# Two shared blocks' gate products moved into the units of the last sequence, and the gather indices computed first

## The reference, cut to what matters

```python
x = x + xattn(layernorm(x), ctx)          # 16 sequences of 128 channels x 512
# xattn: 8 heads of 16, keys within 64 places of the query, softmax, out projection, relu,
#        times ctx, mixing of the channels
xt = layernorm(x)                         # 2048 tokens (rows) of 512
top2 of softmax(xt @ Wr.T + bias)         # 16 experts, weights normalised
routed = sum over the two experts e of w * (silu(xt @ Wg[e]) * (xt @ Wu[e])) @ Wd[e]
shared = silu(xt @ sWg) * (xt @ sWu) @ sWd
out = x + routed + shared
```

## Time and profile before

| what | value |
|---|---|
| median of 3 runs | 713.51 us (709.81 to 713.77) |
| the profiled execution's own time | 713.82 us |
| its span, first to last instruction | 712.1 us |
| TensorE busy | 656.3 us, 92% of the span |
| GpSimd, VectorE, ScalarE busy | 432.8, 390.1, 358.8 us |
| TensorE's mean granted clock | 0.976 of full speed |

### The profile page before, as it was taken

The page is one execution under the profiler, slowest core; times in us unless marked ns, Lnnn a source line. Parts: engine busy times, 40 slices in busy tenths (PEclk is TensorE's granted clock), DMA queues, the critical chain, the costliest instruction groups (busy, mean ns, idle before and its releaser), DMA issues. The chain is left out here.

```text
span 712.1 us, 13863 instructions
## 1 busy us (share of the span) xinstructions
PE 656.3 (92%) x4070; PEld 318.3 (45%) x4070; DVE 390.1 (55%) x1424; ACT 358.8 (50%) x673; POOL 432.8 (61%) x653
## 2 busy tenths in 40 slices
PE   3679999999999999998899999899999999999992
PEld 1345545555555555554444444333333333333330
DVE  3778888888888888861224786322222222222220
ACT  4237777777777777665323101344444344444441
POOL 5238788888888887777310001257867677767663
PEclk9968999999999999998999999999999999999997
DMA  6533545655444444311498944435555566544430
GB/s 204 161 105 91 143 123 164 167 161 151 129 133 139 135 137 137 103 49 50 127 401 342 418 161 149 133 78 108 118 132 107 147 121 128 119 96 88 80 50 0
DMA packets 67579, 99.45 MB, mean 140 GB/s; under 512 B 18601, under 2 KB 43305, under 8 KB 65449
## 3 DMA queue, kind: packets, MB, share of 16 engines
q1 hardware_dynamic: 52848, 70.68, 32.0%
q0 software_dynamic: 9600, 18.89, 14.4%
q10 hardware_dynamic: 5058, 8.99, 3.7%
HBM read 50.99 MB, written 23.33 MB: 104 GB/s over the span
## 5 line engine op out<-in xcount | busy, mean ns | idle before, releaser
L1175 DVE CUSTOM_DVE_ANT_0 bank<-bank,cb 128x192 f32<-128x192 f32 (+1 forms) x512 | 185.8, 415 | 35.5 <-PE bank L580 35.1
L954 ACT ACTIVATE wgu<-bank 128x384 f32<-128x384 f32 (+1 forms) x256 | 125.7, 548 | 45.8 <-PE bank L598 45.2
L785 PE MATMUL bank<-wgu,rowsT 128*64 x320 | 145.9, 599 | 0.0
L787 PE MATMUL bank<-X,rowsT 128*64 128x512 f32 x320 | 145.9, 598 | 0.0
L1408 DVE TENSOR_TENSOR act_in<-act_in,bank 128x256 f32<-128x256 f32 x56 | 23.5, 420 | 194.9 <-ACT act_in L1070 173.5
L580 PE MATMUL bank<-wgu 96*128 96x192 bf16 (+1 forms) x512 | 96.3, 274 | 19.1 <-DVE wgu L1175 14.4
L466 POOL TENSOR_SCALAR_AFFINE_SELECT wgu<-wgu 128x512 f32<-128x512 f32 (+1 forms) x128 | 74.9, 585 | 49.0 <-ACT wgu L954 49.0
L512 POOL DMA_INDIRECT rows<-xn_rows,gather_i x40 | 44.2, 1106 | 84.5 <-DVE gate_of L1403 58.5
L530 POOL DMA_INDIRECT out<-y_out,scatter x40 | 64.2, 1605 | 37.7 <-DMA out<-y_out,scatter_i 23.1
L530 POOL DMA_INDIRECT out<-y_out,scatter_i x40 | 64.3, 1606 | 30.8 <-issue 22.1
L580 PEld LDWEIGHTS bank<-wgu 96*128 96x128 bf16 x512 | 45.8, 102 | 80.4 <-issue 38.6
(11 more groups left out here) (174 smaller groups left out, 1088.8 us busy)
## 6 DMA issues: line engine op xcount, KB each, us to landing
wgu<-wgu SPq DMA_DIRECT2D x190, 128.0 KB, 2.7
wgu<-w_gu SPq DMA_DIRECT2D x16, 1024.0 KB, 14.1
X<-w_d SPq DMA_DIRECT2D x16, 512.0 KB
out<-y_out ACTq DMA_DIRECT2D x17, 256.0 KB, 4.1
X<-x SPq DMA_DIRECT2D x16, 256.0 KB, 3.3
wgu<-ctx SPq DMA_DIRECT2D x16, 256.0 KB, 3.3
xn_rows<-xn SPq DMA_DIRECT2D x16, 256.0 KB, 2.4
xn_turned<-xn2T SPq DMA_DIRECT2D x16, 256.0 KB, 3.4
```

The lines of the kernel that those rows point to most:

```text
L785: mm(gb[k.buf][0:GROUP, :], rowsT[:, k.buf, c, 0:GROUP], wgu[:, bass.ds(e * 2048 + 512 * c, 512)], start=(c == 0), stop=(c == 3))
L787: last = mm(gb[k.buf][GROUP:P, :], rowsT[:, k.buf, c, GROUP:P], gu_half[:, k.buf, 512 * c:512 * c + 512], start=(c == 0), stop=(c == 3))
L954: nc.scalar.activation(probs[j % 4][:, 2 * half:2 * half + 2, 0:w], s2[half][:].rearrange("p (j c) -> p j c", j=2)[:, :, 0:w], ACT.Exp, sc ...
L1175: last = v.tensor_tensor_reduce(o, o, cb[:, B_MASK + off:B_MASK + off + w], 1.0, MASKED * 2.0, ALU.add, ALU.max, rowmaxes[n % 2][:, h + i, ...
```

## The change

Four gate and up products for each of blocks 0 and 1 go into the units U = 129 to 136, one product behind each unit's own work (`soon_gate_up`), into the two banks `s1`, which the score products have left by then. Their SiLU stands at U = 139 and 140, and their `activate` at U = 140 on VectorE. Units 141 to 158 then drain blocks 2 to 7 as they drained blocks 0 to 5, and take the transposes and the down products of blocks 0 and 1 as well. Behind the units eight shared blocks are left where there were ten. The loads of rows start five units before U = 129. The stores of blocks 0 and 1 are issued at i = 4 and 5 behind DRAIN where block 0's was at 7. The gather indices are computed ahead of `places_and_orders` and have a semaphore of their own, `gather_ready`. The first `turn_rows` of the routed blocks, which stood inside the last `pe_step`, stands behind the last `turn_act`, and the second stands behind the last `down`.

The diff, cut to its core:

```diff
-DRAIN, DRAINED = UNITS * (SEQS - 1) + 20, 6
+DRAIN, DRAINED, SOON = UNITS * (SEQS - 1) + 20, 8, 2
+FIRST_SOON = DRAIN - 11
...
-            pool.wait_ge(tables_ready, 1)
+            pool.wait_ge(gather_ready, 1)
...
             for j in range(AHEAD):
                 gather(j)
+            pool.wait_ge(tables_ready, 1)
             pool.wait_ge(spare_stored, 16)
...
+                if 0 <= U - FIRST_SOON < 4 * SOON:
+                    soon_gate_up(*divmod(U - FIRST_SOON, 4))
+                if DRAIN < U <= DRAIN + 3 * (DRAINED - SOON):
+                    third = (U - DRAIN - 1) % 3
+                    drain_shared((U - DRAIN - 1) // 3 + SOON, third)
+
+            def soon_gate_up(b, c):
+
+                k = Turn(b, 0, 2)
+                if b == 0 and c == 0:
                     pe.wait_ge(rowmax, 2 * UNITS * SEQS)
                     pe.wait_ge(shared_in, 96)
...
+                if c == 0:
+                    pe.wait_ge(rows_in[k.n % 3], 16 * (k.n // 3 + 1))
+                last = mm(s1[b][:], rows[:, k.n % 3, P * c:P * c + P], swgu[:, c, :], start=(c == 0), stop=(c == 3))
...
             def drain_shared(b, third):
 
                 k = Turn(b, 0, 2)
                 if third == 0:
-                    if b == 0:
+                    if b == SOON:
                         pe.wait_ge(exp_ready, 2 * UNITS * SEQS)
+                    if b == SOON + 1:
+                        down(Turn(1, 0, 2), s1[1])
                     half_gate_up(k, 0)
                 elif third == 1:
-                    if b == 1:
+                    if b == SOON:
                         pe.wait_ge(o_copied[0], SEQS)
                         pe.wait_ge(o_copied[1], SEQS)
-                    if b > 0:
+                        turn_act(Turn(0, 0, 2))
+                        turn_act(Turn(1, 0, 2))
+                    else:
                         turn_act(k.plus(-1))
                     half_gate_up(k, 1)
-                elif b > 0:
+                elif b == SOON:
+                    down(Turn(0, 0, 2), s1[0])
+                else:
...
-                if U == DRAIN - 4:
+                if U == FIRST_SOON - 5:
                     act.wait_ge(turned_stored, 48)
                     for k in range(3):
                         load_rows(Turn(k, 0, 2))
...
+            def rows_to_gather():
 
                 dve.wait_ge(table_mm, 4)
                 link(v.tensor_copy(table, rb[:, AT_TABLE:AT_TABLE + TABLE]))
-                part = lambda g: table[:, g * BLOCKS:(g + 1) * BLOCKS]
                 link(v.scalar_tensor_tensor(slot[:, 0, :], part(0), float(P), part(1), ALU.mult, ALU.add))
+                v.tensor_scalar(gather_i[:], slot[:, 0, :], -1.0, 0.0, ALU.add, ALU.max).then_inc(gather_ready, 1)
...
             result(Turn(DRAINED + 5, 0, 2))
+            rows_to_gather()
             places_and_orders()
             routing_tables()
             activate(Turn(DRAINED + 7, 0, 2))
             result(Turn(DRAINED + 6, 0, 2))
-            for k in range(DRAINED + 8, SEQS):
-                activate(Turn(k, 0, 2))
-                result(Turn(k - 1, 0, 2))
-                if k == SEQS - 2:
-                    dve.wait_ge(y_ready, SEQS - 4)
-                    copy_half(Turn(SEQS, 0, 2))
+            dve.wait_ge(y_ready, SEQS - 4)
+            copy_half(Turn(SEQS, 0, 2))
             result(Turn(SEQS - 1, 0, 2))
```

More of the change, by code:

```diff
@@ L879, in _ @@
             turn_act(Turn(SEQS - 1, 0, 2))
+            turn_rows(Turn(SEQS, 0, 2))
+            down(Turn(SEQS - 1, 0, 2))
             turn_rows(Turn(SEQS + 1, 0, 2))
-            down(Turn(SEQS - 1, 0, 2))
             pe.wait_ge(experts_in, 16 * EXPERTS)
@@ L1021, in drain_shared @@
             def drain_shared(i):
+                if i in (-1, 0):
+                    silu(Turn(i + 1, 0, 2), s1[i + 1])
+                if i in (4, 5):
+                    store_shared(Turn(i - 4, 0, 2))
                 b, rest = divmod(i - 2, 3)
-                if rest == 0 and 0 < b < DRAINED:
+                b += SOON
+                if rest == 0 and SOON < b < DRAINED:
                     act_copy(Turn(b - 1, 0, 2))
-                if rest == 0 and 0 <= b < DRAINED:
+                if rest == 0 and SOON <= b < DRAINED:
                     silu(Turn(b, 0, 2))
-                b, rest = divmod(i + 6, 3)
-                if rest == 0 and 3 <= b <= DRAINED + 2:
-                    load_rows(Turn(b, 0, 2))
+                if i == 3:
+                    act_copy(Turn(0, 0, 2))
+                    act_copy(Turn(1, 0, 2))
+                for b, at_i in ((3, -6), (4, -2)):
+                    if i == at_i:
+                        load_rows(Turn(b, 0, 2))
+                b, rest = divmod(i - 3, 3)
+                if rest == 0 and 5 <= b + 5 <= DRAINED + 2:
+                    load_rows(Turn(b + 5, 0, 2))
                 b, rest = divmod(i - 7, 3)
-                if rest == 0 and 0 <= b < DRAINED - 1:
+                b += SOON
+                if rest == 0 and SOON <= b < DRAINED - 1:
                     store_shared(Turn(b, 0, 2))
@@ L1065, in result, with silu @@
                                      scale=gate_of[rows_of, j:j + 1]).then_inc(y_ready, 1)
-            def silu(k):
+            def silu(k, from_bank=None):
+                bank_of = gb[k.buf] if from_bank is None else from_bank
                 act.wait_ge(gu_mm, k.n + 1)
                 after(act, at_mm, k.n - 1)
-                nc.scalar.activation(act_in[:, k.buf, :], gb[k.buf][:, 0:INNER], ACT.Silu).then_inc(silu_ready, 1)
+                nc.scalar.activation(act_in[:, k.buf, :], bank_of[:, 0:INNER], ACT.Silu).then_inc(silu_ready, 1)
             def store_shared(k):
@@ L1239, in drain_shared @@
             def drain_shared(i):
+                if i == 0:
+                    activate(Turn(0, 0, 2), s1[0])
+                    activate(Turn(1, 0, 2), s1[1])
+                if i in (4, 5):
+                    if i == 5:
+                        dve.wait_ge(spare_stored, 16)
+                    result(Turn(i - 4, 0, 2), s1[i - 4])
                 b, rest = divmod(i - 2, 3)
-                if rest == 0 and 0 <= b < DRAINED:
-                    activate(Turn(b, 0, 2))
+                if rest == 0 and SOON <= b + SOON < DRAINED:
+                    activate(Turn(b + SOON, 0, 2))
                 b, rest = divmod(i - 6, 3)
[L1245 to L1248, removed]
+                if rest == 0 and SOON <= b + SOON < DRAINED - 1:
+                    result(Turn(b + SOON, 0, 2), yb[0])
             tb, gb, ab, yb, rb = bank[0:2], bank[2:4], bank[4], bank[5:7], bank[7]
@@ L1390, in routing_chunk, with part, routing_tables @@
                                 ALU.mult).then_inc(hot_ready, 1)
[L1392 removed]
+            def part(g):
+                return table[:, g * BLOCKS:(g + 1) * BLOCKS]
+            def rows_to_gather():
                 dve.wait_ge(table_mm, 4)
                 link(v.tensor_copy(table, rb[:, AT_TABLE:AT_TABLE + TABLE]))
[L1396 removed]
                 link(v.scalar_tensor_tensor(slot[:, 0, :], part(0), float(P), part(1), ALU.mult, ALU.add))
+                v.tensor_scalar(gather_i[:], slot[:, 0, :], -1.0, 0.0, ALU.add, ALU.max).then_inc(gather_ready, 1)
+            def routing_tables():
                 link(v.tensor_scalar(slot[:, 1, :], slot[:, 0, :], 0.0, cf[:, C_SPARE:C_SPARE + 1],
                                      ALU.is_equal, ALU.mult))
[L1400 removed]
                 v.scalar_tensor_tensor(scatter_i[:], slot[:, 0, :], -1.0, slot[:, 1, :], ALU.add, ALU.add)
@@ L1403, in routing_tables, with activate @@
                 v.tensor_tensor(gate_of[:], slot[:, 2, :], part(4), ALU.add).then_inc(tables_ready, 1)
-            def activate(k):
+            def activate(k, from_bank=None):
+                bank_of = gb[k.buf] if from_bank is None else from_bank
                 dve.wait_ge(silu_ready, k.n + 1)
-                v.tensor_tensor(act_in[:, k.buf, :], act_in[:, k.buf, :], gb[k.buf][:, INNER:2 * INNER],
+                v.tensor_tensor(act_in[:, k.buf, :], act_in[:, k.buf, :], bank_of[:, INNER:2 * INNER],
                                 ALU.mult).then_inc(act_ready, 1)
```

10 lines of the change are left out of this document (4 added, 6 removed).

## The result

The change measures 707.68 us (median of 7 runs, 704.87 to 708.30) against 713.51 us before (7 runs, 709.69 to 714.38). The ratio is 0.992, with a 95% interval from 0.989 to 0.995: 5.8 us or 0.8% faster. The profiled execution took 707.80 us, its span is 706.1 us.

A forecast was written before the change was run, and what follows sets the result against it. TensorE's work, left equal by the change, was taken to bound the stages. The profiled 713.82 us less 2.8 for filled waits and 3.2 for the clock gave 707.8 us, range 705 to 712.

The forecast's parts named there:

- Waits filled, 2.8 us: In units 129 to 144, moved products fill TensorE's waits: 2.21, 0.24 and 0.31 us, taken as 2.8 us gained.
- the transfer of the maxima: TensorE's 1.09 us wait at 325.36 us: sent by work ahead of unit 129, so not itself pushed.
- The clock, 3.2 us: At 326.34 to 334.24 us, TensorE's clock of 0.59 no longer falls: 3.2 us gained, bounds 0 and 3.2.
- the first rival: The clock falls anyway, in its old place or at later waits: 711.0 us; chance 0.22 together with another rival.
- the waits of 0.95 and 0.31 us: Second window, router at 350.36 us and mixing: similar gaps left the clock at 1.00, so it would stay up.
- The tail: Behind the last router: two blocks, 10.74 us, leave the stretch, 64.28 to 53.54 us, and nothing is lost.
- The landing: First gather in the tail: taken as 4.9 us from its start near 433.5, at most 6.8, costing nothing.
- The indices' own worth, 4.0 us: In the tail: indices left in their old place would let the first gather land at 442.4, 4.0 us late.
- Routers left waiting: Router at 350.36 us: its 0.95 us wait stays, since ScalarE's copy stands behind that unit's SiLU.
- The third rival: More is gained: waits of 0.95 and some of the routed blocks' 2.81 us may go; 705.4 us, chance 0.15.

The follow-up runs named there:

- five fillers: Kernel before plus five products nobody reads, behind units 129, 130, 131, 142 and 151, no work moved: 711.24 us, ratio 0.996.
- before again: The kernel before, unchanged, run once more: 713.91 us, ratio 0.999.
- three fillers: Kernel before plus three products nobody reads, behind the work of units 129, 130 and 131, no work moved: 712.99 us, ratio 0.999.
- all waits: The SiLU behind the copy kernel, early products at other units, ScalarE's block 15 copy ahead of block 14's store: 703.60 us, ratio 0.988; repeat 704.89 us.
- SiLU behind the copy: The change with the drained blocks' SiLU and activate one unit later, behind ScalarE's router copy and VectorE's logits: 704.08 us, ratio 0.986 against before.
- only the tail: Kernel before with only the early indices, their own semaphore and the moved gathered transposes, nothing in the units: 715.52 us, ratio 1.001.

## Why the prediction was right

The forecast was 707.8 us, the measurement 707.68. Part of this is luck: the terms sum to 6.0 us, the stages between unit 129 and the routed blocks of the first two profiled executions give 6.6, and the start and the end, which the change hardly touches, took back 1.1 and gave 0.5. The sum also starts from the profiled 713.82 us, 0.3 above the median that it is held against. With spans that vary by 4 us, 0.1 us of agreement says little; the terms say more. Point by point:

- **Waits filled, 2.8 us.** Right, slightly small. Units 129 to 140 gained 24.57 + 6.86 - 25.22 = 6.2 us; less 3.4 of clock it is 2.8, where 2.21 + 0.24 = 2.45 were forecast. The later stage gained 42.27 + 3.88 - 45.75 = 0.4 us, forecast 0.31. That the transfer of the maxima is not pushed held: its wait was simply covered.
- **The clock, 3.2 us.** The mechanism is shown at its place by the twelve windows: products that nobody reads, put into the waits, take the slow stretch away there as the real ones do. The size was near the upper end: 1.7 to 3.4 us in the four executions with open waits. In whole times it is shown less well: five fillers gain 2.7 us, three gain 1.0 with an interval that takes in nothing, and in the profiles of both a slow stretch came later. Against the first rival, the clock fell in neither of the change's own two executions, nor in any of the four of its variants that keep the early products where the waits are, from 322 to 386 us.
- **A premise that was not safe.** The clock was taken to stay up because the waits of 0.95 and 0.31 us had left it at 1.00 in the second window. In before again and in three fillers it fell behind these very waits. In the change and its variants, where a wait of 1.05 us stands in that place or is gone, it did not fall in the six executions just named; why, no run shows. So it came true that the clock stays up, but the reason given for it is weak.
- **Slow stretches elsewhere.** These the forecast did not have. The stretch at 326 us was there in every execution with the waits open, and only its price varied. But from 290 to 320 us both executions of the change have slow stretches that neither of the kernel before has, worth 3.3 and 1.8 us of clock. They are part of the 1.1 us that the start took back. So the 3.2 us came at their place, and how much of them is left over the whole kernel is less sure than the forecast had it. The Trainium skill ("TensorE: Matmul & The Clock Gate", Part 1) says that the point of a change of clock differs from run to run. The traces agree for the start, but at 326 us the place was decided by the waits.
- **Waits not filled.** The waits of 0.48 and 0.44 us ahead of units 138 and 140 stayed open in the change; they were not in the sum, and in the kernel with all waits, which fills them, the stretch was 0.7 and 1.2 us shorter.
- **The tail.** Right: 53.54 us were forecast for the stretch behind the last router, 53.55 measured; the gather started 1.12 us behind the indices, at 433.6 on the old axis, forecast 433.5. The landing, 4.1 us as the median of three gathers and at most 3.88 for the first, is under the 4.9 taken. It is over the 2.6 estimated from the Trainium skill ("DMA: Bandwidth & Descriptors", Anatomy of one DMA).
- **The indices' own worth, 4.0 us.** The mis-sized term, though no part of the sum: late, they cost 6.1 us in the trace. The landing was 0.5 us longer than taken, and the slow clock behind a long wait, 1.7 us, was left out.
- **Routers left waiting.** Right that the 0.95 us would stand (1.05), and the run with the SiLU behind the copy shows the cause given for it. The third rival had counted on waits going that the change does not touch; they did not go.

What stays open: why the slow stretch at 326 us costs 1.7 us in one execution and 3.4 in another (1.7 in the two that have one at 290 to 320 us as well, 3.4 in the two that have none), why those at 290 to 320 us come with the change, why the waits of 0.95 and 0.31 us are followed by one only sometimes, and what makes the length of the start vary.

## What to carry to other kernels

Where TensorE's work is fixed, work moved to a place gains the waits that it fills, and the clock that falls behind a cluster of them can be worth as much again: 2.8 and 3.4 us here. Products that nobody reads can gain the second alone: five of them 2.7 us (0.8 to 4.6), three of them nothing clear of the noise, since the slow stretch can come behind the next open wait. Before shortening a stage that covers a serial chain of another engine, put that chain on the old time axis: here taking two blocks out of the tail was free only because the gather's indices left early, and each half of the change gained nothing without the other (ratios 1.001 and 0.999). Where spans vary by 4 us in code that nobody changed, compare the lengths of stages, not the totals.

## What was not expected

A gather issued together with other transfers was in place 5.4 us after its start, against at most 3.9 us ahead of them, and GpSimd's instruction for it took 2.10 us instead of 1.31. The clock also fell at 290 to 320 us in every kernel built on the change or its tail, and in no other, though the code there is that of before but for three loads of rows, and in the kernel with only the tail not even these moved. A wait of 5.48 us of TensorE left its clock at 0.62 over the next 4.40 us. And with three waits filled the slow stretch turned up behind the next open ones, of 0.95 and 0.31 us, in one execution of three fillers and also in one of before (0.97 from 336 to 386 us in both).
